# Embedding gathers that wait for TensorE's turn counter

## The reference

```python
sparse_embed = emb_tables[field_idx[None, :], x_sparse]           # (1024, 26, 64)
z = sparse_embed.reshape(B, 26 * 64)
gram = jnp.einsum('bik,bjk->bij', sparse_embed, sparse_embed)
inner = gram[:, iu, ju]                                           # 325 pairs i < j
dnn_in = jnp.concatenate([x_dense, z, inner], axis=-1)            # 2002 columns
h = jax.nn.relu(dnn_in @ w1 + b1)                                 # w1: 2002 x 2002
out = jax.nn.sigmoid(h @ w2 + b2)
```

## Time and profile before

| | us |
|---|---|
| median of three executions | 561.79 |
| the profiled execution | 564.22 |
| its span, first to last instruction | 562.4 |
| TensorE matmul busy | 451.2 (80%) |
| VectorE busy | 345.7 (61%) |
| ScalarE busy | 263.2 (47%) |
| GpSimd busy | 215.4 (38%) |
| mean granted TensorE clock | 0.895 of 2.4 GHz |

### The profile page before, as it was taken

How to read it: one execution, slowest core, us unless ns; L and a number is a source line. 1 busy time by engine, 2 the same in 40 slices (tenths; PEclk the granted TensorE clock), 3 DMA queues, 4 the chain that set the end, 5 groups by cost and what they waited for, 6 DMA issues and landing times.

```text
span 562.4 us, 6304 instructions
## 1 busy us (share of the span) xinstructions
PE 451.2 (80%) x2121; PEld 369.0 (66%) x2121; DVE 345.7 (61%) x835; ACT 263.2 (47%) x412; POOL 215.4 (38%) x215
## 2 busy tenths in 40 slices
PE   7002058798896997889699789948999999999996
PEld 7002047587674876678587578726888888888885
DVE  5001036569772985877576469726878799686432
ACT  3001046556563674665245455335547658443321
POOL 6777607643473677267207633770000000000000
PEclk9656569799997999799799699967999999999999
DMA  8535228885893787457257355535455544736500
GB/s 269 145 27 99 26 74 243 264 265 159 259 340 108 239 220 233 120 130 219 57 183 176 80 157 158 144 61 166 145 190 176 155 164 119 229 117 211 176 1 0
DMA packets 27327, 88.67 MB, mean 158 GB/s; under 512 B 7680, under 2 KB 7688, under 8 KB 27296
## 3 DMA queue, kind: packets, MB, share of 16 engines
q1 hardware_dynamic: 20640, 81.45, 43.6%
q0 software_dynamic: 6656, 6.83, 11.1%
HBM read 88.25 MB, written 0.00 MB: 157 GB/s over the span
## 4 chain that ended last, share of the span: by engine, by line
PE 49%; another core or an unknown queue 16%; DVE 13%; issue 8%; ACT 7%; DMA 5%; SPq 1%; ACTq 0%; DVEq 0%
PE acc L433 15%; PE acc L434 14%; PE acc L418 14%; DVE w_lo L556 6%; PE side L386 5%; ACT w_hi L467 4%; DMA w_raw<-in_L_rec_w_dram 4%; DVE gram L588 2%; DVE pair_u L576 1%; ACT pair_z L481 1%; DVE tail L605 1%; PE side L369 1%; DMA w_raw<-in_L_rec_b_dram 1%; DVE square L598 1%
## 5 line engine op out<-in xcount | busy, mean ns | idle before, releaser
L334 POOL DMA_INDIRECT z<-in_L_rec_emb_tables_dram,idx x208 | 214.5, 1031 | 163.6 <-PE side L369 94.8
L433 PE MATMUL acc<-w_hi,x_hi 128*128 128x500 f32 (+3 forms) x512 | 213.4, 417 | 73.8 <-issue 38.0
L556 DVE TENSOR_TENSOR w_lo<-w_raw,w_hi 128x500 fp32r<-128x500 f32 (+4 forms) x288 | 195.4, 735 | 53.7 <-ACT w_hi L467 42.1
L434 PE MATMUL acc<-w_lo,x_hi 128*128 128x500 f32 (+3 forms) x512 | 207.0, 404 | 7.1 <-issue 7.0
L467 ACT CAST w_hi<-w_raw 128x1002 fp32r<-128x1002 f32 (+3 forms) x128 | 155.8, 1241 | 59.0 <-PE acc L418 34.2
L433 PEld LDWEIGHTS acc<-w_hi,x_hi 128*128 128x128 f32 (+1 forms) x512 | 101.3, 198 | 101.6 <-issue 81.5
L418 PE MATMUL acc<-w_hi,x_lo 128*128 128x500 f32 (+3 forms) x512 | 146.2, 398 | 9.5 <-issue 8.7
L418 PEld LDWEIGHTS acc<-w_hi,x_lo 128*128 128x128 f32 (+1 forms) x512 | 99.0, 194 | 34.2 <-issue 12.8
L434 PEld LDWEIGHTS acc<-w_lo,x_hi 128*128 128x128 f32 (+1 forms) x512 | 101.7, 199 | 26.1 <-issue 7.9
L473 ACT CAST x_hi<-side 128x512 fp32r<-128x512 f32 (+3 forms) x35 | 16.7, 477 | 124.8 <-remote 96.5
L563 DVE TENSOR_TENSOR x_lo<-side,x_hi 128x512 fp32r<-128x512 f32 (+3 forms) x35 | 19.2, 552 | 82.5 <-ACT x_hi L473 43.4
(11 more groups left out here) (40 smaller groups left out, 136.4 us busy)
## 6 DMA issues: line engine op xcount, KB each, us to landing
w_raw<-in_L_rec_w_dram SPq DMA_DIRECT2D x90, 501.0 KB
w_raw<-in_L_rec_w_dram SPq DMA_DIRECT2D x30, 1001.0 KB
z<-in_L_rec_emb_tables_dram,idx POOLq DMA_INDIRECT x208
w_raw<-in_L_rec_w_dram SPq DMA_DIRECT2D x6, 250.5 KB
w_raw<-in_L_rec_w_dram SPq DMA_DIRECT2D x2, 500.5 KB
w2b<-in_L_rec_w_dram SPq DMA_DIRECT2D x1, 501.0 KB
w2b<-in_L_rec_w_dram SPq DMA_DIRECT2D x1, 500.0 KB
w_raw<-in_L_rec_w_dram SPq DMA_DIRECT2D x6, 50.9 KB
```

Source lines behind the costliest of these rows:

```text
L334: pool.indirect_dma_start(out=z[:, t % 2, K * f:K * (f + 1)], out_offset=None, in_=emb_rows, in_offset=bass.IndirectOffsetOnAxis(ap=idx[:, ...
L433: nc.tensor.matmul(o, hi, wh, start=k == 0, stop=False)
L434: nc.tensor.matmul(o, hi, wl, start=False, stop=False)
L556: last = nc.vector.tensor_tensor(w_lo[0:rows, lo + a:lo + z], w_raw[0:rows, of + a:of + z], w_hi[0:rows, lo + a:lo + z], ALU.subtract)
```

## The change

Before each gather POOL may now wait for `w_used`. The number is the turn of the batch's transposes in `PLAN`, less 5 for tile 0 and less 7 for the others, plus one for every two field pairs inside the batch. Where that is zero or negative there is no wait. The wait for `transposed` stays.

```diff
     XS = 4
+
+    AHEAD = (5, 7)
 
@@ in the block of gpsimd
                         pool.wait_ge(transposed, count("TX", ("T", t - 2, gone)))
                     for f in range(2 * first, 2 * (first + n)):
+
+                        turn = int(PLAN[t][0][q]) - AHEAD[t > 0] + (f // 2 - first) // 2
+                        if turn > 0:
+                            pool.wait_ge(w_used, turn)
                         pool.indirect_dma_start(
```

## The result

The changed kernel took 538.80 us (median of four executions, 532.89 to 544.57), the kernel before 561.43 (four, 555.57 to 562.68): a ratio of 0.953, with a 95% interval of 0.946 to 0.960. I had forecast 474, with 447 to 521. So the sign was right and the size was not: 23 us came back of the 88 that I had worked out. The ratios of this document leave out a kernel's slower executions, while medians and ranges take in all of them, so the two can differ by a few per cent. The profiled execution took 541.23 us and has a span of 539.4, so its spans compare with the 562.4 of before.

What follows compares the result with a forecast made beforehand. Long runs of GpSimd gathers were taken to hold back TensorE's completions until slice 27, with TensorE itself the bound from slice 29; 562.4 - 41 - 22 - 33 + 8 = 474.4 us of span, forecast 474, range 447 to 521.

Steps and rivals of the forecast that it cites:

- Part 1: Start: a GpSimd pause at 26.3 lets the first cast start at 29.2, turn 1 at 34.9 instead of 76.0; -41 us.
- the 2.9 us: Start: assumed delay from GpSimd's pause to TensorE's first word, taken from a later run of about this length; bounds 1.6 to 6.4.
- Part 2: Turns 1 to 31: a stuck word stops GpSimd after four gathers, bounding the delay; two thirds of 33 us come back, -22.
- rival A: Waits free the start alone; GpSimd lags behind the counts, runs stay long, later stages stay unchanged; 521 us, chance 0.20.
- Part 3: Turns 32 to 71: stalls and cold restarts hold 41 us; four fifths come back, -33, bounds 0 and 41.
- Part 4: Turns 72 to 111: gathers of tiles 6 and 7 now fall here and TensorE may wait for them; +8, at worst 27.
- C: Whole kernel: waits cut every run so well that nothing stalls and nothing is added; 447 us, chance 0.20.
- B: Start: TensorE's words are held by something other than gathers; nothing gained, late gathers waited for; 582 us, chance 0.05.
- the first gap: Start: TensorE's first transpose issues at 12.64, yet ScalarE starts only at 41.20, while GpSimd issues 23 gathers.
- D: Whole kernel: the change does not bite, counts always past when GpSimd asks; 562 us, chance 0.03.

Runs made afterwards that it cites:

- the pause after every eighth: Kernel before, with GpSimd waiting after every eighth gather until the batch's gathers so far have landed: 491.22 us, ratio 0.856.
- even spacing: Changed kernel with its wait counts laid out evenly, two gathers a turn: 488.43 us; again on another chip 487.20 us, ratio 0.859 to the kernel before.
- the third set: Follow-up runs on one chip: gather form against row addresses, even spacing, rarer pauses; the kernel before took 568.66 us there.
- the first half alone: Changed kernel with the new waits for tiles 0 and 1 only: 454.41 us (kernel before 454.11); on another chip 552.09 us (before 559.31).
- longer leads: Changed kernel with 11 turns ahead instead of 7 for tiles 1 to 7: 553.37 us, ratio 0.988 to the kernel before.
- indirect, consecutive: Kernel before with the same 208 indirect DMAs reading consecutive table rows: 565.27 us, beside 568.66 for the kernel before.
- the second half alone: Changed kernel with the new waits for tiles 2 to 7 only: 465.19 us, ratio 1.042; on another chip 570.78 us (kernel before 567.58).

## Why the prediction was right and wrong

**The mechanism: right, and narrower than I said.** "During a long run of gathers TensorE's completions reach the others late, and a pause of GpSimd lets them through." Breaking the runs takes 14% off the kernel before (the pause after every eighth), and taking away the indirect form takes 19 to 20%. But runs of DMAs as such don't do it, only those of indirect ones issued by GpSimd, and only on some chips: of the four on which I ran experiments one shows none of it.

The trace has the late word itself, in its records of semaphore updates. TensorE's first transpose ends at 12.91 in the kernel before, and the increment of `transposed` is recorded at 41.17, 0.03 us before ScalarE's cast. Matched with the last such instruction that had ended, TensorE's increments are over 1 us late 40 times there, up to 29.1 us; 46 times and up to 17.4 in the changed kernel, 31 times and up to 6.7 with even spacing (28 times and up to 10.2 in the third set), 21 times and up to 3.7 with the pause after every eighth. In the traces of plain DMAs and of the chip without stalls none is. So short runs make the delays short; they don't end them.

On the chip without stalls the first cast is at 12.45 (the first half alone). On the others eight traces have the same first eighteen gather instructions, and their first casts come at 41.2 (before), 25.7, 23.6 and 13.8 (the changed kernel), 23.5 (longer leads), 20.7 and 19.6 (its halves) and 16.1 (indirect, consecutive). When a word gets through in mid-run is by chance, as far as these traces tell.

**Part 1, the start (forecast -41, measured -46): the size fits by luck.** GpSimd pauses at 26.4 as foreseen, but the first cast starts at 23.64, ahead of it. The second cast at 29.54 does fall in the pause. (The run behind which I had read the 2.9 us was of 16 gathers, not 17.) In three executions of the changed kernel turn 1 starts at 30.1, 18.0 and 31.6, and in the second of them no wait held GpSimd: it issued 50 gathers in a row up to 73.4. Without the first wait turn 1 starts at 76.0, 30.1 (the second half alone) and 21.8 (indirect, consecutive). The 76.0 from which I subtracted was the latest start of them all, and that the first wait makes turn 1 earlier isn't shown. And I took the gain to be final. It is not: the second half alone also starts turn 1 at 30.1 with no wait there, and has given nearly all of it back by turn 32 (220.8, against 228.4 before). A better mark is the start of turn 32. The waits for tiles 0 and 1 alone reach it at 217.5, the whole change at 190.3, 178.6 and 194.6. The start seems to be worth something only if what stands behind it is lighter too.

**Part 2, turns 1 to 31 (forecast -22, measured +7.8): the step that failed.** I wrote that the new waits "bound the delay", that "GpSimd stops by itself" when TensorE's word is stuck. For that its counts must be near the turn that TensorE is in. They are not: 26 gathers need 33 to 35 us (1.27 to 1.33 each), and the counts of a tile span only five to seven turns. At the undisturbed pace of a turn that is 27 to 31 us in turns 1 to 31 (138.5/31 = 4.5 each) and 16 to 19 later (125.6/40 = 3.1). So GpSimd starts a tile on its wait, falls behind, and finds each later count long met. The trace of after has this for tile 2: the turn of its first count ends at 99.3 and its first gather starts at 100.4, but the turn of its last count, 22, ends at 119.5 and that gather starts at 129.2. Where I had foreseen "many short waits of 1 to 3 us", 109 of the 149.3 us are four long pauses (37.7, 37.4, 19.7 and 14.5), and the runs between pauses are of 18, 16, 18 and 30 gathers before 145 us and of up to 26 later. Five pauses of 2.0 to 4.4 us, 16 together, are the stops on a stuck word that I had counted on: they end 4 to 18 us after the turn asked for had ended. They stand behind runs of 12 to 30 gathers, and not of four. This is what rival A said ("GpSimd lags behind the counts once it is running"). I gave it 0.20, and I had the numbers for it in my own text. The bound that I did have in the trace, 12 us of a run without harm, I did not hold against the 33 to 35 us that a tile's gathers take.

The longer leads do not settle this step: their 29 us are lost at the start, in part, and where more gathers now stand. Even spacing tests it: two gathers a turn, 13 turns a tile, which is 40 us at 3.1 each and so more than the 33 to 35 that GpSimd needs. It has 29 pauses of over 1 us, the changed kernel on that chip 13, and from turn 32 on its longest run is of 18 gathers, where that has one of 26. It won 57 us.

**Part 3, turns 32 to 71 (forecast -33, measured -11.8).** It failed with part 2, and what came back can be put down to gathers that left: 52 are in it instead of 78. With the cost per gather of before, 41/78 = 0.53 us, the 26 that left are worth 13.7. So the waits as such gained nothing here. The even layout, with 63 gathers in it, takes 132.0.

**Part 4, turns 72 to 111 (forecast +8, measured +26.9).** The late gathers are worth what I said: on the chip without stalls the stage goes from 121.0 to 129.5, 8.5 us. The rest, 18 us, is stalls and their cold restarts; I had taken those to be cured. "At worst the 52 gathers cost what gathers cost in part 3", 27, was the value measured: the waits did not lower what a gather costs. (On the other two chips that stall the stage takes 146.7 and 142.5.)

So by this account, which is argued from the costs per gather and from the halves, the change works as a transfer. It takes 34 gathers out of the start and 26 out of turns 32 to 71, puts 8 more into turns 1 to 31 and 52 into turns 72 to 111, which had none, at about half a us each, and gains before turn 32. There both halves are needed: one alone reaches turn 32 at 217.5 or 220.8, both together at 178.6 to 194.6. The rivals: A had the mechanism, but took parts 2 to 4 as unchanged (521); with the move of the 52 gathers, -13.7 + 27, it gives 534 and comes near 539. C (447) would have needed short runs. B is out: the first gap does depend on GpSimd, since with plain DMAs the first cast comes at 12.5. D is out by the ratio; on the chip without stalls it would be the other way round, for there the waits of tiles 2 to 7 cost 11 us by the medians and have nothing to give (the whole change did not run on it).

The section "Issuing engines are not separate DMA queues" of the Trainium skill's "DMA: Bandwidth & Descriptors" says that transfers of all engines end up on the same 16 DMA engines, and that the choice of issuer only saves sequencer time. Plain DMAs from GpSimd agree: 453.72 and 453.75 us, no stall. Indirect ones don't: the same packets cost 105 to 115 us more, in a place that the DMA engines' busy share doesn't show.

**Open.** Why the indirect form holds TensorE's completions, and why on some chips only. ScalarE's own increments are never over 0.01 us late in these traces, and of DVE's at most four in a trace are late by over 1 us, up to 4.8. Open too is whether the word alone is held or TensorE as well, which goes from instruction to instruction slowly while a stall lasts (see below). And the rival that I could not test: every execution here had its instructions recorded, and the recording itself may take part in the stalls. The records hint at a tie: traces with stalls hold 3300 to 4300 records of semaphore updates, those without some 6750, on the chip without stalls and with plain DMAs on the others alike. Most of those missing are landings of DMAs, of SyncE's as well as of the gathers. So it isn't shown that a kernel whose instructions are not recorded would stall, or gain by even spacing.

## What to carry to other kernels

A wait that is to cap a producer's run caps it only if the count is still unmet when the producer gets there: work out the issue time of the group (26 x 1.33 us) against the time that its counts span, and spread the counts over all of it. A gain at one stall is not a gain at the end until what stood behind it has been looked at; ask what the producer will run into next. A stall that ends by chance can't be priced from one trace: look at the same stretch in several executions before a forecast subtracts from it. And where one engine's completions arrive late while DMA is half idle, look at what another engine is issuing, and try the same transfers in another form before trying to time them.

## What the runs showed of the hardware

An indirect DMA of 128 rows holds GpSimd for 1.03 us and the next follows 0.30 behind it; a plain one with the same packets holds it for 0.54. Waiting for a group's landing costs 3.7 us a time (183.0 in 50) behind every fourth gather and 4.3 (102.4 in 24) behind every eighth. A chip matters more than the change: the kernel before took 454 us on one and 559 to 569 on the other three. While a stall lasts TensorE is not dead: it advances by an instruction every 0.7 or 1.4 us (141.23, 141.96, 143.36, 144.06 in the trace of after; where 1.4 us lie between two, a record may be missing), and each of the first three is 0.37 us long. The granted clock can also fall without a stall: with plain DMAs on a chip that stalls it is 0.50, the lower level of 1.2 GHz, from 140 to 160 us, with TensorE busy for 20.00 us of these 20, behind 10 us in which it was busy for 8.26 at 0.94.
